# Neighbour sums of a graph layer in two levels: 32-column one-hots in four column strips, then units added per tile

## The chip, the cores and the metric

The kernel runs on one core of one Trainium2 chip. The metric is the device time of one execution in microseconds (us), as a median over runs. A core has a matrix engine (TensorE, rows marked PE; its weight loads are marked PEld), a vector engine (VectorE, DVE), a scalar engine (ScalarE, ACT), GpSimd (POOL), which also issues the indirect DMAs, and a sync engine (SP) that issues plain DMAs. The engines run their own streams in order and meet at semaphores.

## The reference, cut to what matters

There are N = 6250 nodes with D = 512 features, and E = 100000 edges whose `dst` is sorted. With `xn` the layer norm of `x`:

```
deg = max(segment_sum(1, dst), 1)
agg = segment_sum(xn[src], dst)                  # the part that changes
gnn = xn @ W1.T + b1 + (agg / deg) @ W2.T + b2
mix = linear attention over all nodes (16 heads): relu(q), relu(k), v, then a projection
x   = x + gnn + mix
x   = x + ffn(layernorm(x))                      # 2 of 8 experts, chosen once for all nodes
```

## The kernel before

Nodes are worked in T = 49 tiles of 128 rows. Numbers are carried as pairs of fp16 (a high part and a low part), so a product of two pairs is three fp16 matmuls for each 128 of the contraction (`three`: the high weights times high and low of the other side, lines L549 and L550, then the low weights times high, L554). A matmul here has 128 x 128 stationary values and 512 moving columns unless told otherwise.

**The first stage** (loop `for i in range(-1, T + 2)`, called the K stage below) normalizes the tiles, stores each one's fp16 pair as 128 rows of 2 KB to a table in HBM, and computes the attention's keys and a 512 x 512 sum: 12 + 12 matmuls a tile (`three` for the key, L708 to L710 for the sum). Preparation work of the weights and the edge lists is put between its iterations by `STEPS`. One of these steps, `below`, counts for every tile which block of 128 edges is its first one.

**A short middle** builds the attention's matrix from that sum (L759 to L772).

**The layer stage** runs `layer(i)` for i = 1 to 51. Iteration i holds the query of tile i (L742, L743, L747), for tile i-1 the transposes (L793 and L800), `three` with `wg1`, `three` with `wg2` (these take the tile's aggregate) and `three` with `wm`, and for tile i-2 the transpose of the new normalized row (L838). That makes 48 matmuls of 512 columns and 12 transposes a tile. It also holds the aggregation of a tile `ahead = i + skew`; skew is 3 at first and falls to 0 (`LAYERS`), as iterations without an aggregation are put in. Tiles 0 to 2 are aggregated in the K stage (`EARLY`: i = 39, 42, 45) and tile 3 in the middle.

**The expert stage** follows and is not touched.

**The aggregation.** GpSimd gathers the edges' source rows from the table: one indirect DMA for each block of 128 edges (`fetch`, L522), 784 of them, into a ring of R = 16 slots of 128 x 1024 fp16. SP waits for the slots' DMAs and passes each four on as `arrived`. VectorE makes one-hots of 128 edges x 128 nodes, four blocks at a time (`one_hot`, L1238: is the edge's `dst` the node's number?). TensorE multiplies: `add` is two matmuls for each block, one-hot times high half (L622) and low half (L623), into `ps_agg` (bank 6), all blocks of a tile into the same 128 x 512 sums. A block with edges of two tiles is multiplied in both. A `group` of four blocks ends with a matmul of one column (`nothing`, L610) that carries a semaphore; when it is done, GpSimd may fill the four slots again (`released`). The sum's last column is the degree (each table row ends in a constant): VectorE takes its reciprocal (`degrees`, L1268 and L1271), and ScalarE copies the scaled sum to SBUF (`keep_ah`, L961).

The gathers begin when the last table row is stored. The ring is the only thing that lets GpSimd run ahead of TensorE.

Of the kernel before, what the change touches and what calls it, by code (L numbers as in the profile page):

```python
# [16 lines left out]
ALU = mybir.AluOpType  # L17
# [14 lines left out]
U = 4  # L32
NULL = U // 2
COLS = (NULL + BLOCKS + (E % P == 0) + R - 1) // R * R
ROUNDS = COLS // R
RG = R // U
OG = 6
GROUPS = COLS // U
CH = (BLOCKS + P - 1) // P
FULL = BLOCKS // P  # L40
XI = 6
NS = 4
# [30 lines left out]
def after(eng, sem, count):  # L73

    if not isinstance(count, int) or count > 0:
# [8 lines left out]
EARLY = {39: 0, 42: 1, 45: 2}  # L84
LAYERS = ((1, 4, 3), (4, 12, 3), (12, 13, None), (13, 24, 2), (24, 25, None), (25, 36, 1), (36, 37, None), (37, T, 0),
          (T, T + 3, None))

# [7 lines left out]
STEPS.update({15: [("dst", 0), ("dst", 1)], 16: [("src", 0), ("src", 1)], 17: [("below", 0)]})  # L95
# [12 lines left out]
def raw_read(t):  # L108

    s = t + OFF  # L110
    if t >= T - NS:
        return 0
    for k, first in enumerate(RAW):
        if k and first <= s < first + C:
            return ORDER.index((k, C - 1)) + 1
    return ORDER.index(("below", 0)) + 1 if EDGES <= s < RAW[G2] else 0


def layers(eng, body):

    for lo, hi, skew in LAYERS:
        a, b = -(-lo // SLOTS), hi // SLOTS
        if lo < 4 or b <= a:
            a = b = hi // SLOTS + 1
        for i in range(lo, min(a * SLOTS, hi)):
            body(i, skew, i % SLOTS)
        if b > a:
            with eng.Fori(a, b) as g:
                for k in range(SLOTS):
                    body(g * SLOTS + k, skew, k)  # L130
            for i in range(b * SLOTS, hi):
                body(i, skew, i % SLOTS)


def program(nc, x, src, dst, gw1, gb1, gw2, gb2, qkv_w, proj_w, proj_b, attn_w, attn_b, gate_w, gate_b,
            w1, b1, w2, b2, out):
    ctx = ExitStack()
    with ctx:
# [3 lines left out]
        table = nc.dram_tensor("table", (N, 2 * D), F16, kind="Internal").ap()  # L142
        x2_dram = nc.dram_tensor("x2_rows", (ROWS, D), F32, kind="Internal").ap()
# [15 lines left out]
        below = edges[:, 4 * CH * P:].bitcast(F16)[:, 0:CH * (T + 1)].rearrange("p (a f) -> p a f", a=CH)  # L159
# [18 lines left out]
        firsts, uns = ring32[:, 15, 0:T + 1], ring32[:, 15, T + 1:2 * (T + 1)]  # L178
        before = ring32[:, 15, 2 * (T + 1):2 * (T + 1) + CH].bitcast(I32)
# [3 lines left out]

        onehot = sb("onehot", [P, OG * U, P], F16)
        oh32 = onehot[:, :, :].rearrange("p a f -> p (a f)").bitcast(F32)
        plb = oh32[:, 0:C * P].rearrange("p (a f) -> p a f", a=C)
# [1481 lines left out]
```

## Time and profile before

| | |
|---|---|
| median of 3 runs | 1579.8 us (1578.48 to 1582.28) |
| the profiled execution's span | 1578.3 us |
| TensorE busy | 1519.8 us (96%) |
| GpSimd busy | 799.0 us (51%), 753.5 us of it gathers |
| VectorE, ScalarE busy | 1003.1 us (64%), 604.5 us (38%) |
| mean DMA rate | 196 GB/s |

The profile gives no separate time of its own for the profiled execution beside its span. The span lies 1.5 us under the median, and I treat that as what lies around it. "Busy" of an engine is the time covered by its instructions. A matmul is shown with its full length from first column in to last column out (about 0.38 us), while the next one starts about 0.2155 us after it, so a busy TensorE need not be a full one: distances between starts tell more.

### The profile page before, as it was taken

The numbers are of one execution on the slowest core, as the hardware profiler recorded it, in microseconds if no ns is written. First come the engines' busy times: TensorE is split into PE (matmuls) and PEld (weight loads), VectorE is DVE, ScalarE is ACT, GpSimd is POOL, SyncE is SP. The second block draws the span as 40 slices with busy tenths as digits, with TensorE's granted clock in tenths as the row PEclk, the third lists the DMA queues.
The fourth block names the chain that finished last, engine by engine and source line by source line (L and its number), as shares of the span: only waits on it lengthen the run. The fifth ranks groups of instructions, "written<-read, shape, count | busy, mean of one in ns | idle before, by whom it ended". The sixth has DMA issues, their size and how long they took to land.

```text
span 1578.3 us, 29172 instructions
## 1 busy us (share of the span) xinstructions
PE 1519.8 (96%) x7597; PEld 733.7 (46%) x7598; DVE 1003.1 (64%) x2154; ACT 604.5 (38%) x997; POOL 799.0 (51%) x847
## 2 busy tenths in 40 slices
PE   5999999989999999999999999999999989999997
PEld 2444444444544444444444444444544444444443
DVE  7576522246666667666677666666666666666777
ACT  5777721111333333332333333333333335555554
POOL 4122143646777767777767777767777710000000
PEclk8999999999999999999999999999999989999998
DMA  9977776957777767777767777767777723322323
GB/s 237 262 170 190 189 179 132 217 151 208 234 235 234 234 209 231 234 234 237 233 206 239 239 240 233 234 209 236 236 233 233 233 80 120 107 90 96 106 87 112
DMA packets 166610, 308.64 MB, mean 196 GB/s; under 512 B 71986, under 2 KB 74572, under 8 KB 166260
## 3 DMA queue, kind: packets, MB, share of 16 engines
q0 software_dynamic: 62720, 205.57, 44.3%
q1 hardware_dynamic: 36112, 58.90, 11.7%
q10 hardware_dynamic: 67684, 42.96, 10.7%
q8 instruction: 53, 0.87, 0.2%
q14 instruction: 41, 0.34, 0.1%
HBM read 255.02 MB, written 39.49 MB: 187 GB/s over the span
## 4 chain that ended last, share of the span: by engine, by line
PE 70%; POOL 14%; issue 6%; DVE 3%; DMA 1%; ACT 0%; DVEq 0%; SPq 0%; ACTq 0%
POOL ring L522 14%; PE bank L549 13%; PE bank L554 13%; PE bank L550 12%; PE bank L622 8%; PE bank L623 8%; PE bank L708 2%; PE bank L709 2%; PE bank L710 2%; PE bank L742 2%; PE bank L747 2%; PE bank L743 2%; PE bank L793 1%; PE bank L838 1%; PE bank L800 1%
## 5 line engine op out<-in xcount | busy, mean ns | idle before, releaser
L522 POOL DMA_INDIRECT ring<-table,src_col x784 | 753.5, 961 | 328.9 <-issue 254.5
L622 PE MATMUL bank<-ring,onehot 128*128 x830 | 316.1, 381 | 14.8 <-issue 6.2
L623 PE MATMUL bank<-ring,onehot 128*128 x830 | 315.5, 380 | 0.0
L1238 DVE TENSOR_TENSOR onehot<-bank,dst_col 128x512 f32 x244 | 168.8, 692 | 96.5 <-issue 61.1
L961 ACT ACTIVATE work<-bank,rd 128x512 f32<-128x512 f32 x49 | 33.7, 687 | 336.4 <-DVE rd L1271 336.3
L549 PE MATMUL bank<-wts,xT 128*128 128x512 f16 x392 | 149.1, 380 | 4.1 <-DVE wts L1313 4.1
L550 PE MATMUL bank<-wts,xT 128*128 128x512 f16 x392 | 149.0, 380 | 0.0
L549 PE MATMUL bank<-wts,work 128*128 128x512 f16 x392 | 148.2, 378 | 0.2 <-DVE work L1441 0.2
L550 PE MATMUL bank<-wts,work 128*128 128x512 f16 x392 | 148.3, 378 | 0.0
L622 PEld LDWEIGHTS bank<-ring,onehot 128*128 x830 | 80.9, 97 | 126.5 <-issue 45.6
L623 PEld LDWEIGHTS bank<-ring,onehot 128*128 x830 | 81.1, 98 | 84.8 <-issue 0.9
L554 PE MATMUL bank<-wts,xT 128*128 128x512 f16 x392 | 101.5, 382 | 0.0
L554 PE MATMUL bank<-wts,work 128*128 128x512 f16 x392 | 100.6, 379 | 0.0
L1052 ACT ACTIVATE std<-mv,epsc 128x1 f32<-128x1 f32 x49 | 14.4, 295 | 222.6 <-DVE mv L1437 222.6
L1268 DVE TENSOR_SCALAR dg<-bank 128x1 f32<-128x1 f32 x49 | 7.7, 158 | 137.2 <-PE bank L610 137.2
L1118 ACT ACTIVATE work<-work 128x512 f32<-128x512 f32 x98 | 61.8, 630 | 79.9 <-DVE work L1622 78.8
L509 POOL TENSOR_TENSOR work<-work 128x512 f16<-128x512 f32 x27 | 31.7, 1176 | 119.8 <-ACT work L1015 119.8
L1013 ACT ACTIVATE work<-bank 128x512 f32<-128x512 f32 x49 | 29.2, 596 | 136.0 <-PE bank L554 131.6
L1622 DVE SCALAR_TENSOR_TENSOR work<-bank,mix,work 128x512 f32<-128x512 f32 x98 | 69.9, 747 | 15.1 <-PE bank L554 9.8
L1612 DVE SCALAR_TENSOR_TENSOR ring<-work,gexp,ring 128x512 f32 (+1 forms) x98 | 73.3, 748 | 8.9 <-DVE ring L1612 3.8
L549 PE MATMUL bank<-xT,wts 128*128 (+2 forms) x208 | 75.0, 367 | 3.1 <-ACT wts L1096 3.1
L708 PE MATMUL bank<-work,xT 128*128 128x512 f16 x180 | 69.6, 386 | 6.0 <-POOL work L509 6.0
(284 smaller groups left out, 2732.5 us busy)
## 6 DMA issues: line engine op xcount, KB each, us to landing
ring<-table,src_col POOLq DMA_INDIRECT x784, 3.7
x_rows<-work ACTq DMA_DIRECT2D x49, 256.0 KB, 3.7
work<-in_x ACTq DMA_DIRECT2D x48, 256.0 KB, 4.3
ring<-x_rows SPq DMA_DIRECT2D x12, 1024.0 KB, 5.3
out_x<-ring SPq DMA_DIRECT2D x12, 1024.0 KB
table<-xT SPq DMA_DIRECT2D x45, 256.0 KB, 3.5
ring<-in_x SPq DMA_DIRECT2D x42, 256.0 KB, 3.7
xT<-in_L_mix_qkv_weight SPq DMA_DIRECT2D x2, 1024.0 KB, 10.1
```

Source lines behind the costliest of these rows:

```text
L522: pool.indirect_dma_start(ring[:, n, :], None, table[:, :], bass.IndirectOffsetOnAxis(ap=ap, axis=0)).then_inc(slot_loaded[n], 16)
L549: mm(out_, wh(c), mh(c), start=first and c == 0, stop=False)
L550: mm(out_, wh(c), ml(c), start=False, stop=False)
L554: r = mm(out_, wl(c), mh(c), start=False, stop=last and c == n - 1)
L622: mm(ps_agg[:, :], w[:, k, :], rows[:, k, 0:D], start=start, stop=False, skip_group_check=True)
L623: r = mm(ps_agg[:, :], w[:, k, :], rows[:, k, D:2 * D], start=False, stop=stop, skip_group_check=True)
L708: mm(bank[c][:, :], xs[:, c * P:(c + 1) * P], kh, start=(t == 0), stop=False)
L961: F(ah[:, k % SLOTS, :], ps_agg[:, :], ACT.Copy, scale=rd[:]).then_inc(s["ah_made"], 1)
L1118: F(act2[:, j % 2, e], pre[:, j % 2, e], ACT.Gelu).then_inc(s["act_made"], 1)
L1238: V.tensor_tensor(onehot[:, bass.ds((q + t) % OG * U, U), :], ps_iota[:, None, :].to_broadcast([P, U, P]), dst_col[:, bass.ds(q % GROUPS * ...
L1612: r = V.scalar_tensor_tensor(out=y, in0=act2[:, j % 2, e], scalar=gexp[:, e:e + 1], in1=y, op0=ALU.mult, op1=ALU.add)
L1622: V.scalar_tensor_tensor(out=pre[:, j % 2, e], in0=bank[4 + 2 * (j % 2) + e][:, :], scalar=mix[:, 4:5], in1=b2b[:, e], op0=ALU.mult, op1=A ...
```

## The change

The blocks' sums are made in two levels. Blocks are taken three at a time as a *window* (384 edges; about 24 nodes by the mean degree of 16). `base[w]` is the first node of window w, and a one-hot is 128 edges x 32 nodes, relative to that base. Four windows (12 blocks) make a *unit*; there are 66 units. Window j of a unit uses column strip j of TensorE's array: its one-hot is 32 stationary columns at column 32 j, and its sums go to partitions 32 j to 32 j + 31 of `ps_unit` (bank 7). A *step* is one block of each of the four windows: two passes (high, low) of four matmuls, 197 steps in all (195 of four blocks, 2 of one). Three steps fill a unit. ScalarE then copies it to SBUF as the high fp16 half, VectorE makes the low half, into one of 6 unit slots. A tile's sum is then made from the 2 to 4 units that can hold its nodes (16 tiles have 4, 32 have 3, one has 2; 162 in all), with 128 x 128 one-hots (`keys`) that match node numbers: two matmuls for each unit, into the same `ps_agg` as before.

What else it does: the lists of first blocks and the loops with bounds read at run time go, `layer` is unrolled, and SP no longer relays arrivals (TensorE waits on one of four semaphores per step). The steps begin in the K stage at i = 33, one in each iteration (18 of them), 6 are put into the middle, and 173 into the layers by a plan (`PLAN`) at five places of each. Tiles 0 to 2 are summed at i = 40, 46 and 48 of the K stage. Skew falls to 0 at layer 23 instead of 37. The gathers of step n wait for step n-4. 782 blocks are gathered, not 784. The preparation step `below` gives way to three steps `first`, with a list built by VectorE (`make_lists`). If the lists are unsorted or spread too far (a window over more than 32 nodes, or a first node over 48 from its even place), the kernel takes a slower way first (`slow_tiles`). The descriptor memory of GpSimd's DMAs is set to 4096 bytes in place of its default of 16384.

What that test reads in the inputs: `dst` is sorted, the widest gap between first nodes of windows is 28, and the largest distance from the even place is 18. So the slower way is not taken.

```diff
-U = 4
+LANES, DEEP, WIDE = 4, 3, 32
+RG = R // LANES
+UB = LANES * DEEP
+UNITS = (BLOCKS + UB - 1) // UB
+STEP = P * DEEP * N // E // 8 * 8
+SPREAD = LANES * STEP
+DRIFT = 48
+HOLD = 6
-EARLY = {39: 0, 42: 1, 45: 2}
-LAYERS = ((1, 4, 3), (4, 12, 3), (12, 13, None), (13, 24, 2), (24, 25, None), (25, 36, 1), (36, 37, None), (37, T, 0),
+FIRST = 33
+TILES_K = {40: 0, 46: 1, 48: 2}
+LAYERS = ((1, 12, 3), (12, 13, None), (13, 17, 2), (17, 18, None), (18, 22, 1), (22, 23, None), (23, T, 0),
           (T, T + 3, None))
+def units_of(t):
+    lo = max(0, -(-(P * t - DRIFT - SPREAD) // SPREAD))
+    return range(lo, min(UNITS - 1, (P * t + P - 1 + DRIFT) // SPREAD) + 1)
 # in step_plan, the count of steps at place p (0 to 4) of layer i; n steps are out already
+            if t is not None and p < 3:
+                count = -(-(need - n) // (3 - p))
+            else:
+                count = 1 if n < more else 0
 # GpSimd
-            for b in range(COLS):
-                if b % U == 0:
-                    pool.wait_ge(s["released"], b // U + 1)
-                fetch(b % R, src_col[:, b:b + 1])
+            for n in range(STEPS_SUM):
+                u, k = divmod(n, DEEP)
+                after(pool, s["step_done"], n - RG + 1)
+                for j in lanes_of(n):
+                    b = UB * u + DEEP * j + k
+                    fetch(slot(n, j), src_col[:, b:b + 1], step_loaded[n % RG])
 # TensorE
-            def group(q, t, part=None, f=None):
...
+            def add_step(n):
+                u, k = divmod(n, DEEP)
+                last = n + 1 == steps_to(u)
+                pe.wait_ge(step_loaded[n % RG], 16 * sum(len(lanes_of(m)) for m in range(n % RG, n + 1, RG)))
+                if k == 0:
+                    pe.wait_ge(s["hot_made"], u + 1)
+                    after(pe, s["unit_lo"], u)
+                for h in range(2):
+                    for j in lanes_of(n):
+                        a = j * WIDE
+                        r = mm(ps_unit[a:a + WIDE, :], hot[:, u % 2, DEEP * j + k, :], ring[:, slot(n, j), h * D:(h + 1) * D],
+                               start=(k == 0 and h == 0), stop=(h == 1 and k == DEEP - 1 or last), skip_group_check=True,
+                               tile_position=(0, a))
+                r.then_inc(s["step_done"], 1)
+            def add_units(t):
+                us = units_of(t)
+                after(pe, s["ah_made"], t)
+                after(pe, s["dg_made"], t)
+                pe.wait_ge(s["keys_made"], t + 1)
+                pe.wait_ge(s["unit_lo"], us[-1] + 1)
+                for j, u in enumerate(us):
+                    mm(ps_agg[:, :], keys[:, t % 2, j, :], units[:, u % HOLD, 0:D], start=(j == 0), stop=False)
+                    r = mm(ps_agg[:, :], keys[:, t % 2, j, :], units[:, u % HOLD, D:2 * D], start=False, stop=(u == us[-1]))
+                r.then_inc(s["agg_made"], 1)
 # ScalarE
+            def unit_high(u):
+                act.wait_ge(s["step_done"], steps_to(u))
...
+                F(units[:, u % HOLD, 0:D], ps_unit[:, :], ACT.Copy, scale=SU).then_inc(s["unit_hi"], 1)
 # VectorE
-                V.tensor_tensor(onehot[:, bass.ds((q + t) % OG * U, U), :],
-                                ps_iota[:, None, :].to_broadcast([P, U, P]),
-                                dst_col[:, bass.ds(q % GROUPS * U, U), None].to_broadcast([P, U, P]),
-                                ALU.is_equal).then_inc(s["oh_made"], 1)
+            def make_hot(u):
...
+                V.tensor_tensor(hot[:, u % 2, 0:w, :], iota16[:, None, 0:WIDE].to_broadcast([P, w, WIDE]),
+                                rel_col[:, b:b + w, None].to_broadcast([P, w, WIDE]), ALU.is_equal
+                                ).then_inc(s["hot_made"], 1)
+            def make_keys(t):
+                after(dve, s["agg_made"], t - 1)
+                for j, u in enumerate(units_of(t)):
+                    r = V.tensor_scalar(keys[:, t % 2, j, :], iota16[:], tile_base[:, t:t + 1], node[:, u:u + 1],
+                                        ALU.add, ALU.is_equal)
+                r.then_inc(s["keys_made"], 1)
+            def unit_low(u):
+                dve.wait_ge(s["unit_hi"], u + 1)
+                V.scalar_tensor_tensor(out=units[:, u % HOLD, D:2 * D], in0=ps_unit[:, :], scalar=SU,
+                                       in1=units[:, u % HOLD, 0:D], op0=ALU.mult, op1=ALU.subtract).then_inc(s["unit_lo"], 1)
+                if u + 2 < UNITS:
+                    make_hot(u + 2)
```

## Rows read from the trace of the kernel before

**Rows 1.** The page's costliest groups: the gathers and one of the aggregation's two matmul lines.

```profile
L522 POOL DMA_INDIRECT ring<-table,src_col x784 | 753.5, 961 | 328.9 <-issue 254.5
...
L623 PE MATMUL bank<-ring,onehot 128*128 x830 | 315.5, 380 | 0.0
```

**Rows 2.** Line L522's summary: durations in ns and starts in us; then its idle.

```profile
L522 POOL DMA_INDIRECT ring<-table,src_col x784: 940/946/1447, 209.1 to 1268.5; - x196
...
  issue: 254.5, 764
  PE bank L610: 72.5, 14
  PE bank L623: 1.8, 6
...
DMA to landing us min/median/max: 3.3/3.7/8.6
```

**Rows 3.** GpSimd's instructions in order of time, K stage: start, duration, idle before.

```profile
209.14 1.12 POOL L522 DMA_INDIRECT ring<-table,src_col  x1 [22.09 <-issue]
...
253.12 0.94 POOL L522 DMA_INDIRECT ring<-table,src_col  x1 [23.06 <-PE bank L610]
254.36 0.94 POOL L522 DMA_INDIRECT ring<-table,src_col  x1 [0.30 <-issue]
```

**Rows 4.** TensorE in order of time, one layer of the steady stage.

```profile
706.75 0.19 PE L610 MATMUL bank<-ones,zero 128*128 128x1 f16 x2
706.80 0.63 PE L793 MATMUL bank<-ident,work 128*128 128x128 f32 x4
707.27 0.60 PE L800 MATMUL bank<-ident,work 128*128 128x128 f32 x4
707.73 0.39 PE L622 MATMUL bank<-ring,onehot 128*128 x1
...
711.22 1.03 PE L554 MATMUL bank<-wts,xT 128*128 128x512 f16 x4
712.08 0.38 PE L622 MATMUL bank<-ring,onehot 128*128 x1
```

**Rows 5.** Summary of line L1379, once for each tile.

```profile
L1379 DVE SCALAR_TENSOR_TENSOR work<-bank,ksb x49: 681/691/692, 349.8 to 1270.8; 128x512 f32<-128x512 f32 x49
```

**Rows 6.** Busy time by stretch: engines, granted clock, DMA share, GB/s.

```profile
core 0: us, PE busy (x) PEld busy (x) DVE busy (x) ACT busy (x) POOL busy (x), PEclk, DMA share, GB/s
...
340.00:358.00 18.00, 11.81 (x49) 5.20 (x47) 9.85 (x27) 3.11 (x5) 13.74 (x15) 1.00 0.72 207
...
520.00:1160.00 640.00, 634.95 (x3289) 311.82 (x3288) 435.43 (x958) 201.91 (x303) 472.33 (x494) 1.00 0.76 231
```

**Rows 7.** TensorE in order of time at the start of layer 1.

```profile
358.74 0.63 PE L623 MATMUL bank<-ring,onehot 128*128 x1
359.17 0.63 PE L622 MATMUL bank<-ring,onehot 128*128 x1
```

**Rows 8.** ScalarE in order of time: the key's copy, iterations 33 and 34 of the K stage.

```profile
220.93 0.60 ACT L1013 ACTIVATE work<-bank 128x512 f32<-128x512 f32 x1 [4.09 <-PE bank L554]
226.11 0.60 ACT L1013 ACTIVATE work<-bank 128x512 f32<-128x512 f32 x1 [4.09 <-PE bank L554]
```

**Rows 9.** Groups by line and shape, 520 to 1160 us: busy, mean ns, idle before.

```profile
L1238 DVE TENSOR_TENSOR onehot<-bank,dst_col 128x512 f32 x152 | 105.2, 692 | 59.1 <-issue 37.5 <-DVE bank L1246 12.8 <-PE bank L610 5.6
...
L1444 DVE SCALAR_TENSOR_TENSOR work<-bank,work 128x512 f16<-128x512 f32 x34 | 23.1, 681 | 0.0
...
L961 ACT ACTIVATE work<-bank,rd 128x512 f32<-128x512 f32 x31 | 21.3, 687 | 223.5 <-DVE rd L1271 223.5
```

**Rows 10.** Summary of line L1268, which ends each tile's aggregation.

```profile
L1268 DVE TENSOR_SCALAR dg<-bank x49: 147/159/160, 271.3 to 1277.6; 128x1 f32<-128x1 f32 x49
```

**Rows 11.** VectorE and GpSimd in order of time, steady stage.

```profile
677.89 0.74 DVE L1486 SCALAR_TENSOR_TENSOR work<-work,e 128x512 f32<-128x512 f32 x1
678.30 1.15 POOL L522 DMA_INDIRECT ring<-table,src_col  x1 [0.30 <-issue]
```

More of the change, by code:

```diff
@@ L41 @@
 XI = 6
+HOLD = 6
+SU = 2.0 ** -8
 NS = 4
@@ L115, in raw_read @@
             return ORDER.index((k, C - 1)) + 1
[L116 to L132, printed above, removed]
+    return ORDER.index(("first", 2)) + 1 if EDGES <= s < RAW[G2] else 0
 def program(nc, x, src, dst, gw1, gb1, gw2, gb2, qkv_w, proj_w, proj_b, attn_w, attn_b, gate_w, gate_b,
@@ L529, in _, with fetch @@
[L529 to L530 removed]
+            many = slow_tiles(pool)
+            def fetch(k, ap, sem):
+                pool.indirect_dma_start(ring[:, k, :], None, table[:, :],
+                                        bass.IndirectOffsetOnAxis(ap=ap, axis=0)).then_inc(sem, 16)
+            with pool.If(many > 0):
+                with pool.Fori(0, many) as t:
                     with pool.Fori(0, ROUNDS) as g:
[L532 to L533 removed]
+                        it = t * ROUNDS + g
+                        pool.wait_ge(s["slow_half"], it * 2 + 1)
@@ L801, in layer @@
                     r.then_inc(s["turned_p"], 1)
-                if ahead is not None:
-                    with pe.If(a + 1 < b):
-                        group(a + 1, ahead)
-                t = i - 1
+                steps_at(1)
                 if real(t):
                     after(pe, s["x2_made"], t)
-                    if isinstance(t, int) and t == 0:
+                    if t == 0:
                         pe.wait_ge(s["matrix_split"], 2)
@@ L839, in layer @@
                     r.then_inc(s["turned_x2"], 1)
-            layers(pe, layer)
+            for i in range(1, END):
+                layer(i)
             warm(3)
@@ L932, in prepare @@
             def prepare(n, kind, c):
-                if kind in ("scale", "below"):
+                if kind in ("scale", "first"):
                     act.wait_ge(s["steps_act"], n)
@@ L1437, in layer @@
                     V.bn_aggr(mv, st6[:]).then_inc(s["mv2_made"], 1)
+                for u in ends(i, 0):
+                    unit_low(u)
                 t = i - 1
@@ L1477, in layer @@
                     weigh(t)
+                for u in ends(i, 1, 2):
+                    unit_low(u)
                 t = i - 2
```

640 lines of the change are left out of this document (359 added, 281 removed).

## The prediction

> **What bounds the kernel now.** I read the page first: its share of busy time says TensorE (96%), with 1660 matmuls of the aggregation (two lines of 830) as the largest term [rows 1]. Then I looked at how GpSimd issues its gathers, since they feed these matmuls. A gather is shown with 0.946 us and is followed by 0.30 us of "issue", so they come every 1.25 us even when nothing holds them [rows 3]. Over all, (753.5 + 254.5 - 22.1) / 784 = 1.2575 us each [rows 1, 2]; the 22.1 us is the idle time ahead of the first one [rows 3]. The waits on TensorE (lines L610 and L623) are only 72.5 + 1.8 = 74.3 us in total [rows 2]. Check: 209.1 + 784 x 1.2575 + 74.3 = 1269.3, and the last gather starts at 1268.5 and takes 0.95 [rows 2].
>
> So there are two bounds, one just behind the other. TensorE needs 19.19 us a tile ((1270.8 - 349.8) / 48, rows 5 being one event for each tile: [rows 5]). GpSimd needs 782 / 49 = 15.96 blocks x 1.2575 = 20.07 us a tile. GpSimd is the slower one in the steady stage, where it is never held, and lives on the lead it has from the K stage. The lead is small because of the ring: 16 gathers from 209.1, then 23 us of waiting for tile 0's aggregation [rows 3], and so on three times more.
>
> What is to be seen: taking matmuls from TensorE is worth, in this kernel, at most the 74 us in which GpSimd waited, and not the time of the matmuls.
>
> **The change: TensorE's work.** Matmuls of 512 columns start 0.2155 us apart: four of L554 take from 711.22 to 712.08 [rows 4]. A tile has 48 of them, 10.34 us, and 12 transposes: L793's four and L800's take 0.47 and 0.46 us to the next start [rows 4], with L838's as many, 1.4 us. The aggregation is 830 / 49 x 2 = 33.9 matmuls [rows 1], 7.3 us. Sum 19.1 against the 19.19 measured.
>
> Removed: 1660 x 0.2155 = 358 us, and the one-column matmuls. Added for the units: 162 x 2 x 0.2155 = 70 us, 1.5 us a tile with the wait. Added for the steps: 197 times s, the time of one step. No row shows four matmuls in column strips, so I bound it. Below: the four of a pass run together, 2 x 0.2155 = 0.43 us. Above: they run one after the other, 8 x 0.2155 = 1.72 us. I take **s = 0.8**: two passes, and 0.17 us of refill on either side for the change of shape, by the difference between a matmul's length (0.38) and its pitch (0.2155) [rows 1, 4]. A tile then costs TensorE 10.34 + 1.4 + 1.5 + 4.02 x 0.8 = 16.5 us, which is less than GpSimd's 20.07; 197 x 0.8 + 70 = 228 us replace 358.
>
> The Trainium skill, "TensorEngine Tiling (Array Packing)", Key Properties, says that a change of tiling mode drains TensorE, which speaks against two changes for each step of eight short matmuls; no row here shows one. By "TensorE: Matmul & The Clock Gate", Part 3, three column tiles gave 2.38x; carried to four (an estimate from that page, 3.2x) a pass would take 0.27 us and a step 0.54, and the sum below would be some 9 us lower. The same part says that weight loads overlap matmuls in flight only where their row groups differ; here all four strips use all rows, which would make the strips run in turn (the second rival).
>
> **The change: the other engines.** VectorE loses 152 / 640 x 19.19 = 4.6 one-hots of 0.69 us a tile [rows 9], 3.2 us. It gains 1.33 units x (0.68 for the low half, as L1444, and 0.6 for 12 x 32 one-hots, 384 of L1238's 512 elements) and 3.3 keys, each at most half a one-hot of L1238, 0.34: 2.8 us. It was busy 435.4 of 640 us [rows 6] and stays below. ScalarE gains 1.33 x 0.69 us (as L961, rows 9: [rows 9]) where it was busy 202 of 640 us. Both are hidden by GpSimd's pace. Their place matters: one bank holds the unit in the making, so a unit's first step waits for both copies of the one before, 0.69 + 0.68 and some 0.4 between engines, 1.8 us; but steps lie 5.03 us (four gathers) apart where gathers bound, and that covers it. If TensorE were the bound, 65 x 1.8 us would partly show. The lists cost VectorE some 5 us more at i = 12 to 17, where normalization runs many tiles ahead, so 0. Seven fp32 products of 128 columns on TensorE there cost at most 1.3 us (0.12 to 0.2 each), all ahead of the gathers: **+1.3**. SP's relay goes, worth at most 0.3 us a step where TensorE waits for a gather: inside the landing time below. The smaller descriptor memory changes nothing unless it holds fewer than the four or so gathers in flight (landing 3.7 us over a pitch of 1.25, [rows 2]); then the gathers' pitch would grow, which is part of the third rival.
>
> **The change: when gathers may start.** The first gather moves to 209.1 + 1.3 = 210.4. The K stage's iteration lasts 5.18 us (226.11 - 220.93) [rows 8]. Step 0 comes after the key of tile 33, at 222.2, and later iterations last 5.18 + 0.8 = 5.98 us. Four gathers last 5.03 us, and those of step n wait for step n-4, so the ring's lead of four steps is eaten up at about n = 13. The middle holds six steps in about as much time as it had with tile 3's blocks, and layer 1 starts near 354 (before, matmuls of layer 1 are under way at 358.7, [rows 7]). Step 24 stands late in layer 1: 354 + 3 x 2.6 + 1 + 0.8 = 363.7. Step 28's gathers can't start before it; unheld they would start at 210.4 + 28 x 5.03 = 351.2. **12.5 us** are lost by then, in place of nearly all the 74. After layers 12 and 22, which sum no tile, TensorE has some 18 us of other work between two steps, with a ring of 20 us less 3.7 of landing: 4.0 + 3.5 us lost, and 1.4 in small ones. In sum 21.4. Elsewhere TensorE is the faster (16.5 against 20.07), so it takes each step as it lands.
>
> The last gather ends at 210.4 + 782 x 1.2575 + 21.4 = **1215.1**, against 1269.5 before: 54.4 us earlier.
>
> **The change: behind the last gather.** Before, the last aggregation ended at 1277.6 [rows 10], 8.1 us behind the last gather. Now the plan gives layers 3, 3 and 6 steps in turn, and 6 to layer 46, 3 to layer 47, 0 to layer 48. Layer 46's last step lands 7.5 us before the end of the last gather, plus 3.7: 1211.3. Then step, units and transposes 3.1, layer 47 at TensorE's pace (10.34 + 1.45 + 2.4 + 1.4 = 15.6), and layer 48 up to its units (10.34 + 0.95 + 1.4 = 12.7): 1242.7. That is 27.5 us behind the last gather, so **19 us are given back**. What follows (layers 49 to 51, experts: 1578.3 - 1277.6 = 300.7 us) is the same work in the same order. Span: 1242.7 + 300.7 = 1543.4; with the 1.5 us to the median, **1545 us**, 35 under the 1580 shown.
>
> **The likeliest one's own range.** s = 0.45 takes off 12 us (gather stalls 10 in place of 21, less in the last layers); s = 1.2 adds 20. A gather pitch of 1.2475 (0.946 + 0.30, no contention) takes off 8. So 1526 to 1565.
>
> **Rivals.**
> 1. *The strips are nearly free and gathers smooth*: s near 0.45 and the low pitch, 1526 to 1532. Within the likeliest.
> 2. *The strips run in turn* (the other side). s = 1.72: TensorE then needs 13.3 + 6.9 = 20.2 us a tile, plus the copies' 1.8 us wherever two steps meet across a unit. By the same sum the stalls are 98 us and the end is 1628. This mechanism decides from s = 1.4 on, where it comes to 1578. For it: nothing in the trace shows strips side by side. Against it: TensorE works through the small shapes it has at less than its pitch for 512 columns (one-column matmuls of L610 in pairs within 0.05 us, [rows 4]), so small pieces don't each cost a full slot. Neither settles s. (The rule on weight loads from Part 3 of the TensorE page of the Trainium skill, named above, would bring this about; no row here shows it.) 12 in 100.
> 3. *Gathers grow slower.* A gather is 15 ns over its shortest in the mean, 12 us in all, and a long one (1.15 us) falls beside VectorE's L1486, which reads two SBUF operands [rows 11], as others do. The new one-hots read two SBUF operands; the old ones read PSUM and one. If the excess doubles, +12: 1557; were each new one-hot to hold a gather by its own 0.6 us, 66 x 0.6 = 40 us: 1585. 10 in 100, 1557 to 1585.
> 4. *TensorE's clock falls in the starved layers.* Every third layer has six steps and lasts 29 us with some 18 us of work, idle 3 to 4 us at a time. In 340 to 358 TensorE was busy 11.8 of 18 us, and from 358.4 to 361.7 matmuls started 0.43 us apart, the lower of its two levels (1.2 GHz in place of 2.4) [rows 6, 7]. While it waits for gathers this costs nothing; what reaches into the next two layers, at 15.6 us against 15.1 us of gathers, costs half of such a stretch, 1.7 us, up to 13 times: +22, 1567. 10 in 100.
> 5. *No change*: TensorE's waits (a unit's copies behind long queues on VectorE and ScalarE, 1.5 to 3 us a layer) bring it to 19.2 us a tile again: 1575 to 1583. 6 in 100.
> That the change doesn't run as written (its slower way) is excluded by the inputs.
>
> **Chances.** Likeliest 58 (with rival 1), rival 2 12, rival 3 10, rival 4 10, rival 5 6, and 4 for something slower unnamed. Taking 0.2% (3 us, about what this kernel's runs can tell): faster 58 + 10 + 10 + 2, less 1 for rival 3's upper end, 79; the same 5; slower 16. The range 1522 to 1585 leaves out rival 2 and some 6 more.
>
> **What the new profile should show.** A gather pitch of 1.25 to 1.26 us from 210 on with under 30 us of waits on TensorE in total, most of them before 370; last gather at 1205 to 1225; strips of a pass starting a few ns apart and a step of 0.5 to 1.2 us; TensorE waiting on gathers in every third layer; last `dg` at 1230 to 1255, then 300.7 us. Wrong it would be by a step of over 1.4 us, a pitch over 1.27, or a tail after the last `dg` that isn't 300 us.

## The result and the profile after

The changed kernel takes 1563.95 us (median of 4 runs, 1555.31 to 1565.38), against 1580.96 us for the kernel before, measured beside it: ratio 0.9882, 95% interval 0.9856 to 0.9909. So it is 1.2% faster, where 2.2% was predicted. The profiled execution has a span of 1561.7 us (predicted 1543.4) and took 1563.55.

The page of the changed kernel, its busy shares, its shares of the chain that ended last, the gathers' group that answers to [rows 1], and the group of the steps' matmuls. Columns as there.

```profile
PE 1388.8 (89%) x7490; PEld 619.8 (40%) x7490; DVE 933.8 (60%) x2172; ACT 640.9 (41%) x1063; POOL 799.5 (51%) x849
...
POOL 39%; PE 30%; issue 13%; DVE 3%; DMA 3%; ACT 1%; SPq 0%; DVEq 0%; ACTq 0%; POOLq 0%
...
L609 POOL DMA_INDIRECT ring<-table,src_col x782 | 753.5, 963 | 282.0 <-issue 255.3
...
L724 PE MATMUL bank<-ring,hot 128*32 128x512 f16 x1564 | 127.4, 403 | 123.2 <-DMA ring<-table,src_col 101.3
```

The same chain of the kernel before:

```profile
PE 70%; POOL 14%; issue 6%; DVE 3%; DMA 1%; ACT 0%; DVEq 0%; SPq 0%; ACTq 0%
```

TensorE's busy share fell from 96% to 89%, and the chain that ended last now runs over GpSimd's gathers (39%, 14% before) more than over TensorE (30%, 70% before). TensorE waits 101.3 us for gathered rows, where it waited 2.3 us for SP's word of them before: the bound has passed from one engine to the other.

The summary of the gathers' line of the changed kernel, answering to [rows 2].

```profile
L609 POOL DMA_INDIRECT ring<-table,src_col x782: 940/946/1438, 220.1 to 1232.4; - x196
its engine sat idle before it (us, times) until:
  issue: 255.3, 766
  PE bank L724: 26.7, 16
...
DMA to landing us min/median/max: 3.4/3.8/15.2
```

The waits on TensorE are 26.7 us (74.3 before, 21.4 predicted). Ahead of the first gather lie 22.24 us of idle, so a gather takes (753.5 + 255.3 - 22.2) / 782 = 1.2616 us (1.2575 predicted). The first one starts at 220.1 and not at 210.4.

The summary of the line that ends each tile's aggregation, for the changed kernel, answering to [rows 10].

```profile
L1405 DVE TENSOR_SCALAR dg<-bank x49: 146/158/159, 279.3 to 1261.3; 128x1 f32<-128x1 f32 x49
```

The last gather ends at 1232.4 + 0.95 = 1233.3. The last aggregation comes 28.0 us behind it (27.5 predicted), and 1561.7 - 1261.3 = 300.4 us follow (300.7 predicted).

Busy time in the stretch of [rows 6], changed kernel.

```profile
520.00:1160.00 640.00, 552.40 (x3249) 240.67 (x3242) 392.38 (x967) 225.68 (x344) 481.99 (x501) 0.95 0.78 234
```

TensorE is busy 552 of 640 us (635 before). GpSimd issues 501 gathers in place of 494, 1.4% more: this small number is the whole steady gain. In this stretch the gathers waited 20.5 us on TensorE before (19.3 on L610, 1.2 on L623) and wait 7.2 now; those 13 us are more than the 9 us that seven gathers take. The granted clock is 0.95 in place of 1.00.

TensorE in order of time in one layer, changed kernel, answering to [rows 4].

```profile
453.39 1.03 PE L658 MATMUL bank<-wts,xT 128*128 128x512 f16 x4
454.35 0.61 PE L724 MATMUL bank<-ring,hot 128*32 128x512 f16 x8
454.90 0.66 PE L852 MATMUL bank<-ident,work 128*128 128x128 f32 x4
```

A whole step, eight matmuls of 512 columns in four strips, takes 454.90 - 454.35 = 0.55 us. The estimate worked out from the Trainium skill, "TensorE: Matmul & The Clock Gate", Part 3, by carrying its factor for three column tiles to four, was 0.54, and the trace agrees. Two passes that each take the pitch of one matmul are 2 x 0.2155 = 0.43, so both changes of shape together cost some 0.12 us.

### Where the missing 18 us are

The span is 18.3 us over the predicted one. Term by term, from the rows above: gathers' start +9.7 (220.1 for 210.4), pitch +3.2 (782 x 0.0041), waits on TensorE +5.3, tail +0.5, rest -0.3. Sum 18.4. The largest is the start, which I had put at +1.3 us and which came to +11.0.

ScalarE in order of time, K stage of the changed kernel: L1082 is the key's copy that was L1013. The first five lines are iterations 14 to 18; the last one is iteration 33.

```profile
120.86 0.60 ACT L1082 ACTIVATE work<-bank 128x512 f32<-128x512 f32 x1
129.32 0.60 ACT L1082 ACTIVATE work<-bank 128x512 f32<-128x512 f32 x1 [2.25 <-PE bank L658]
135.26 0.60 ACT L1082 ACTIVATE work<-bank 128x512 f32<-128x512 f32 x1 [2.41 <-PE bank L658]
147.11 0.60 ACT L1082 ACTIVATE work<-bank 128x512 f32<-128x512 f32 x1 [7.23 <-PE bank L658]
152.73 0.60 ACT L1082 ACTIVATE work<-bank 128x512 f32<-128x512 f32 x1 [2.28 <-PE bank L658]
...
231.74 0.60 ACT L1082 ACTIVATE work<-bank 128x512 f32<-128x512 f32 x1 [4.09 <-PE bank L658]
```

The same copies of the kernel before:

```profile
118.59 0.60 ACT L1013 ACTIVATE work<-bank 128x512 f32<-128x512 f32 x1 [0.30 <-PE bank L554]
124.97 0.60 ACT L1013 ACTIVATE work<-bank 128x512 f32<-128x512 f32 x1 [0.17 <-PE bank L554]
130.92 0.60 ACT L1013 ACTIVATE work<-bank 128x512 f32<-128x512 f32 x1 [2.42 <-PE bank L554]
136.30 0.60 ACT L1013 ACTIVATE work<-bank 128x512 f32<-128x512 f32 x1 [0.77 <-PE bank L554]
141.92 0.60 ACT L1013 ACTIVATE work<-bank 128x512 f32<-128x512 f32 x1 [1.73 <-PE bank L554]
```

The lag behind the kernel before is 2.3 us at the first line, 4.3 at the second and third, and then 10.8 at the fourth, where it stays up to iteration 33 (231.74 against 220.93, [rows 8]). Two pieces of work stand at these places. The first is on VectorE:

```profile
113.72 3.17 DVE L1313 TENSOR_SCALAR xT<-ident,xT 128x128 f32<-128x128 f32 x7
117.11 0.75 DVE L1300 SCALAR_TENSOR_TENSOR wts<-bank,scale,wts 128x512 f16<-128x512 f32 x1 [0.21 <-DVE xT L1313]
```

The seven products are 3.17 us long, and the split of the weights stands behind them in VectorE's queue (at 117.11; 114.45 in the kernel before). The second is on TensorE, where the three `first` steps come in one iteration. In order of time, TensorE's wait behind the first piece, and its wait at the second:

```profile
121.90 0.52 PE L698 MATMUL bank<-ident,xT 128*128 128x128 f32 x3 [3.03 <-ACT wts L1003]
...
139.72 0.46 PE L670 MATMUL bank<-xT,ones 128*128 128x128 f32 x2 [3.16 <-ACTq L987]
```

The three matmuls of L698 in the first line start at 119.24 in the kernel before, after 0.25 us of idle. The profile names ScalarE's queue, which acknowledges each such step (L987), as what ended the second wait.

Behind both waits matmuls start 0.43 us apart, the lower of the two clock levels: from 123.1 to 126.5 and from 140.3 to 143.7. In the kernel before they start 0.2155 us apart at these places. Eight such distances cost 1.7 us more than at the higher level. So the lag of 10.8 us is 2.7 us at the first piece and 1.7 us of lower clock behind it, then 4.8 us at the second (the longer products, and the wait) and 1.7 us of lower clock again. This account is read from the start times.

### The profile page after: what moved, and what is told of

The parts are those of the page before. It is cut to its first block, busy times and chain, and to the rows that moved or that the text cites. A ratio compares the mean times of both kernels' runs of the same rounds, so it can differ in the third digit from the quotient of the medians.

```text
span 1561.7 us, 22443 instructions
## 1 busy us (share of the span) xinstructions
PE 1388.8 (89%) x7490; PEld 619.8 (40%) x7490; DVE 933.8 (60%) x2172; ACT 640.9 (41%) x1063; POOL 799.5 (51%) x849
## 3 DMA queue, kind: packets, MB, share of 16 engines
q10 hardware_dynamic: 67684, 42.96, 10.8%
## 4 chain that ended last, share of the span: by engine, by line
POOL 39%; PE 30%; issue 13%; DVE 3%; DMA 3%; ACT 1%; SPq 0%; DVEq 0%; ACTq 0%; POOLq 0%
POOL ring L609 39%; PE bank L653 8%; PE bank L658 8%; PE bank L654 8%; PE bank L776 2%; PE bank L778 2%; PE bank L777 2%; DMA ring<-table,src_col 1%; DMA xT<-awb 1%; PE bank L724 1%; DMA work<-in_x 1%; DVE ring L1754 1%; DVE work L1764 0%; PE bank L737 0%; PE bank L738 0%
## 5 line engine op out<-in xcount | busy, mean ns | idle before, releaser
L609 POOL DMA_INDIRECT ring<-table,src_col x782 | 753.5, 963 | 282.0 <-issue 255.3
L653 PE MATMUL bank<-wts,xT 128*128 128x512 f16 x588 | 234.3, 398 | 6.4 <-DVE wts L1452 3.3
L724 PE MATMUL bank<-ring,hot 128*32 128x512 f16 x1564 | 127.4, 403 | 123.2 <-DMA ring<-table,src_col 101.3
L654 PE MATMUL bank<-wts,xT 128*128 128x512 f16 x588 | 233.8, 398 | 0.0
L658 PE MATMUL bank<-wts,xT 128*128 128x512 f16 x588 | 156.4, 390 | 0.0
L724 PEld LDWEIGHTS bank<-ring,hot 128*32 128x32 f16 x1564 | 24.5, 95 | 209.3 <-DMA ring<-table,src_col 144.0
L658 PE MATMUL bank<-wts,work 128*128 128x512 f16 x392 | 101.3, 381 | 0.0
L1361 DVE SCALAR_TENSOR_TENSOR units<-bank,units 128x512 f16<-128x512 f32 x66 | 45.6, 691 | 78.6 <-ACT units L1013 78.5
L653 PEld LDWEIGHTS bank<-wts,xT 128*128 128x128 f16 x588 | 59.6, 101 | 80.9 <-issue 24.0
L658 PEld LDWEIGHTS bank<-wts,xT 128*128 128x128 f16 x588 | 59.3, 101 | 75.3 <-issue 10.4
L1082 ACT ACTIVATE work<-bank 128x512 f32<-128x512 f32 x49 | 29.2, 596 | 143.0 <-PE bank L658 132.3
L654 PEld LDWEIGHTS bank<-wts,xT 128*128 128x128 f16 x588 | 59.8, 102 | 64.2 <-issue 9.9
L1013 ACT ACTIVATE units<-bank 128x512 f16<-128x512 f32 x66 | 38.7, 586 | 112.9 <-PE bank L724 104.0
```

Source lines behind the costliest of these rows:

```text
L609: pool.indirect_dma_start(ring[:, k, :], None, table[:, :], bass.IndirectOffsetOnAxis(ap=ap, axis=0)).then_inc(sem, 16)
L653: mm(out_, wh(c), mh(c), start=first and c == 0, stop=False)
L654: mm(out_, wh(c), ml(c), start=False, stop=False)
L658: r = mm(out_, wl(c), mh(c), start=False, stop=last and c == n - 1)
L724: r = mm(ps_unit[a:a + WIDE, :], hot[:, u % 2, DEEP * j + k, :], ring[:, slot(n, j), h * D:(h + 1) * D], start=(k == 0 and h == 0), stop=( ...
L1013: F(units[:, u % HOLD, 0:D], ps_unit[:, :], ACT.Copy, scale=SU).then_inc(s["unit_hi"], 1)
```

## The experiments

Theory A, as the expectations call it: the strips run side by side, GpSimd's gathers are the bound of the layers, and the end is start of the gathers + 782 pitches + their waits + tail + 300 us.

### 1. Is it the strips, and is it the gathers?

Each kernel of this part ran once, with one run of the kernel before beside it (1577.22 us).

**All four windows on strip 0.** The sums of the four windows then fall on the same 32 partitions; the count and shape of the matmuls stay.

```diff
-                        a = j * WIDE
+                        a = 0
```

> All four windows of a step use column strip 0 and its 32 partitions instead of a strip each (the sums are then not the reference's); all else as in the changed kernel. Theory A, that strips run side by side and that this is what frees TensorE: matmuls in one strip start 0.2155 us apart, a step takes 1.7 us instead of 0.54, TensorE needs some 20.2 us a tile and becomes the bound; 1625 to 1650 us. Rival, that the gathers set the time whatever a step costs: within 10 us of the changed kernel's 1564.

1661.11 us. TensorE in order of time, this kernel:

```profile
601.88 1.90 PE L724 MATMUL bank<-ring,hot 128*32 128x512 f16 x8
603.71 0.39 PE L653 MATMUL bank<-wts,work 128*128 128x512 f16 x1
```

The step takes 603.71 - 601.88 = 1.83 us in place of 0.55, 3.3 times as long. So four strips do run side by side, and this kernel is what rival 2 described: the gathers now wait 132.1 us on TensorE. The time is 33 us above the 1628 worked out for s = 1.72, and 11 above the 1625 to 1650 expected here; the longer step (1.83) explains a part of it, the rest was not traced.

**Half of the gathers.** Only two of the four lanes of a step are fetched; the other two multiply the same rows again, so TensorE's work is whole, while lanes 2 and 3 are summed from the rows of lanes 0 and 1. (TensorE's wait for a step then counts two lanes; that line is left out below.)

```diff
-                for j in lanes_of(n):
+                for j in lanes_of(n)[0:2]:
...
-ring[:, slot(n, j), h * D:(h + 1) * D],
+ring[:, slot(n, j % 2), h * D:(h + 1) * D],
```

> The changed kernel with only the gathers of lanes 0 and 1 of each step; lanes 2 and 3 multiply the rows of 0 and 1 again, so TensorE's work is the same and the sums are not the reference's. Theory A, that GpSimd's issue of gathers is the bound: 15.5 us a tile are left for TensorE, last aggregation some 200 us earlier or less by the K stage's share, total 1390 to 1440 us. Rival, that TensorE's waits for VectorE and ScalarE (a unit's two copies, queues of the layer) keep the layers near 19 us: 1520 to 1560 us.

1441.83 us, 122 less and 2 above the range expected. TensorE now is the bound: the gathers wait 436.8 us for it. Its aggregations number 23 from 757.0 to 1126.0, so 22 distances of 16.8 us a tile, where I had worked out 16.5 (with the measured step in that sum 15.5, so its other terms were 1.3 us short).

**Half of the gathers in the kernel before**: odd blocks are summed from the rows of the even ones. (The edits to `add` and to SP's waits that belong to this are left out below.)

```diff
-                fetch(b % R, src_col[:, b:b + 1])
+                if b % 2 == 0:
+                    fetch(b % R, src_col[:, b:b + 1])
```

> The kernel before with only every second block gathered; TensorE multiplies the rows of the even slots twice, so its work is the same and the sums are not the reference's. Theory A, two bounds close together: TensorE alone keeps 19.1 us a tile, so 1565 to 1580 us, 0 to 15 under the kernel before. Rival, that GpSimd was the sole bound before: under 1540 us.

1560.54 us against 1577.22 beside it: 4 under the range that two close bounds were given, and far from the rival's 1540. Halving the gathers was worth 17 us before the change and 122 after it: TensorE bound the kernel before, with GpSimd close behind it, and now GpSimd comes first.

**The small descriptor memory in the kernel before.**

```diff
-    nc = _bacc.Bacc("TRN2", target_bir_lowering=False, num_devices=1)
+    nc = _bacc.Bacc("TRN2", target_bir_lowering=False, num_devices=1, dynamic_dma_scratch_size=4096)
```

> The kernel before with the descriptor memory of GpSimd's DMAs at 4096 bytes as in the changed kernel. Theory A, that it holds more than the gathers in flight: gathers keep (busy + issue) / 784 = 1.2575 us, 1577 to 1583 us. Rival, that it is what took the pitch to 1.2616 in the changed kernel: 1.261 or more and 3 us longer waits of TensorE.

1581.21 us; the gather's pitch is (749.3 + 254.7 - 22) / 784 = 1.253 us. So the small memory is not what made 1.2575 into 1.2616.

### 2. The gathers' start and the tail

**Cheap lists**: one product in place of seven, and the third `first` step an iteration later.

```diff
-STEPS.update({15: [("dst", 0), ("dst", 1)], 16: [("src", 0), ("src", 1)], 17: [("first", 0), ("first", 1), ("first", 2)]})
+STEPS.update({15: [("dst", 0), ("dst", 1)], 16: [("src", 0), ("src", 1)], 17: [("first", 0), ("first", 1)], 18: [("first", 2)]})
...
-                for k in range(CH):
-                    link(V.tensor_scalar(steps[:, k, :], ident[:], f_dst[:, k, 0:1], None, ALU.mult))
+                link(V.tensor_tensor(steps, ident[:, None, :].to_broadcast([P, CH, P]),
+                                     f_dst[:, :, 0:1].to_broadcast([P, CH, P]), ALU.mult))
```

> The changed kernel, with the seven products for the step matrices made in one wider product on VectorE, and the third list step of the first group moved one iteration later. Theory A (the gathers set the end, so their late start is paid in full): the first gather goes from 220.1 back to about 210 to 212, the last one ends about 8 to 10 us earlier (1233.3 becomes 1223 to 1225), the time is 1553 to 1556. Rival B (the start is hidden, the tiles' matmuls or the transposes of the first stage set the end): first gather earlier, but the waits of the gathers on TensorE and on the tile inputs grow by the same 8 to 10 us, the time stays at 1561 to 1564. Rival C (the start is not late because of these two edits): the first gather stays at 218 to 220, no change.

1553.43 us, ratio to before 0.9819 (0.9784 to 0.9854). The same places in its trace, VectorE's product, ScalarE's copy of iteration 17, the gathers (a fence for each view):

```profile
113.80 1.09 DVE L1313 TENSOR_TENSOR xT<-ident,xT 128x896 f32<-128x896 f32 x1
```

```profile
138.09 0.60 ACT L1083 ACTIVATE work<-bank 128x512 f32<-128x512 f32 x1 [1.90 <-PE bank L659]
```

```profile
L610 POOL DMA_INDIRECT ring<-table,src_col x782: 943/949/1461, 211.3 to 1220.8; - x196
its engine sat idle before it (us, times) until:
  issue: 254.5, 763
  PE bank L725: 23.2, 19
```

The copy is at 138.09, 9.0 us earlier; the first gather at 211.3, 8.8 earlier. TensorE's first wait is 0.95 us in place of 3.03, the second is gone, and no matmul here starts at the lower clock's distance. What was won at the start came through whole: the last gather is 11.5 us earlier, which is the 8.8 and 3.5 us less of waits on TensorE, less 0.8 us of longer pitch. The time is 10.5 less. By the ratios, 0.9819 against 0.9882, it is 10 us, with intervals that just don't touch; rivals B and C are out by the first gather and the waits, not by the time alone.

**DRIFT 24** in place of 48, so that a tile takes fewer units (130 pairs of key matmuls in place of 162), and layer 46 has three steps, layer 47 six.

```diff
-DRIFT = 48
+DRIFT = 24
...
-                count = -(-(need - n) // (3 - p))
+                count = max(0, -(-(need - n) // (3 - p)))
```

> The changed kernel, with 24 blocks in place of 48 between a tile and the units that it may use, so that the units' plan runs less far ahead: 130 additions of a unit to a tile's sum in place of 162, and the last layer has less to do behind the last gather. Theory A (the end is last gather plus what the last tiles need): gathers start and end as before, the last aggregation is 22 to 25 us behind the last gather in place of 28, the time is 1558 to 1561. Rival B (the plan's shift only moves the waits of the gathers on TensorE, the tail is set by the last layers' own chain): 1562 to 1565. Rival D (fewer steps in late layers lets the gathers' waits on TensorE, 26.7, fall too): 1553 to 1558.

1552.41 us, 0.9812 (0.9795 to 0.9828): 11.5 us less, more than any theory had. In its trace the last gather ends at 1232.4 and the last aggregation is at 1254.3, 21.9 us behind: the tail gives 6.1 (theory A's mechanism), the waits are 27.9 and did not fall (so not theory D's), the span (1553.6) is 8.1 lower, and the rest of the 11.5 is within the spread of the runs: the profiled execution, 1555.38, was the slowest of its four.

**Both.**

> Both edits (cheap lists and 24 blocks of drift). Theory A says that they add, since one moves the gathers' start and the other what follows their end: 1548 to 1552. If one of them is covered by the other's wait (rival B), it is no better than the better one alone, 1553 or more.

1544.44 us, 0.9756 (0.9736 to 0.9776). Better than either theory's time. They add, nearly: -19.5, singly -10.5 and -11.5. In the trace the start is 8.6 us earlier (8.8 alone) and the tail 5.1 shorter (6.1 alone).

**Both, and gathers three iterations earlier**, the rows' norms made at two tiles an iteration from i = 18 so that they are there in time.

```diff
-FIRST = 33
+FIRST = 30
...
-        more = steps_to(units_of(nxt)[-1])
+        more = steps_to(units_of(min(nxt + 1, T - 1))[-1])
```

> Both edits, and the gathers begin after tile 30 of the first stage in place of tile 33, with the rows' sums made at two tiles per iteration so that the lists are there; the plan of the steps looks one tile further. Three iterations of 5.2 us earlier: first gather at 195 to 200. Theory A (the gathers at 1.26 us each, one behind the other, set the end): all of it comes through less what the longer overlap with the first stage costs, 1530 to 1540. Rival B (in the first stage the gathers wait for the tiles' transposes and TensorE, so what starts earlier only waits longer there): the waits within the first stage grow by 10 us or more, and the time is that of the kernel with both edits or above, 1545 to 1555.

1530.16 us, 0.9675 (0.9658 to 0.9691), the fastest. Its gathers and its last aggregation:

```profile
L612 POOL DMA_INDIRECT ring<-table,src_col x782: 940/946/1407, 200.0 to 1203.1; - x196
its engine sat idle before it (us, times) until:
  issue: 239.3, 757
  PE bank L727: 20.8, 25
```

```profile
L1408 DVE TENSOR_SCALAR dg<-bank x49: 150/158/160, 272.6 to 1226.8; 128x1 f32<-128x1 f32 x49
```

The first gather is 11.5 us earlier than with both edits alone (211.5), not the 15.6 of three iterations, and the time 14.3 us less: within theory A's range. The gathers' waits fell from 25.6 to 20.8 us, where rival B had them grow by 10.

### 3. The waits that are left: dealing the steps evenly

The plan gives 3, 3 and 6 steps in turn. A three-step layer frees 12 slots, 15.1 us of gathers, and by my sum takes TensorE slightly longer. So four in each layer might end the waits.

**Even, and ahead of need**: at most 1, 2, 2, 3, 4 steps are out at the five places of a layer, whether needed or not.

```diff
...
-                count = 1 if n < more else 0
+            if not count and n < min(max(more, 4 * (i + 1) + LEVEL), base + (1, 2, 2, 3, 4)[p], STEPS_SUM):
```

> The changed kernel with its steps dealt out evenly: four per layer in place of three, three and six in turn. Theory E (the gathers' 26.7 us of waits on TensorE come from the three-step layers, which free only 12 blocks of the ring in the 16.5 us or more that TensorE needs for a layer, 15.1 us of gathers): these waits fall to 10 to 15 us, what is left being the first stage's, the last gather ends 10 to 15 us earlier, time 1549 to 1555; TensorE's clock in the late layers is no lower than 0.91 since no layer is left waiting for two layers' worth of rows. Rival F (the waits come from the first stage and from the layers without a tile, not from the dealing): waits stay at 22 to 28 us and the time at 1560 to 1565. Rival G (a layer now waits for its fourth step's rows where it waited for three, so the last aggregation comes later than 28 us behind the last gather): above 1565.

1567.83 us, 0.9911 (0.9894 to 0.9927): slower than the changed kernel, though its gathers end sooner.

```profile
L610 POOL DMA_INDIRECT ring<-table,src_col x782: 941/946/1472, 219.0 to 1223.3; - x196
its engine sat idle before it (us, times) until:
  issue: 254.0, 762
  PE bank L725: 18.4, 20
```

```profile
L1406 DVE TENSOR_SCALAR dg<-bank x49: 145/158/159, 278.2 to 1264.6; 128x1 f32<-128x1 f32 x49
```

The last gather ends at 1224.2, 9.1 us earlier, and the last aggregation comes 40.4 us behind it in place of 28.0. So the waits did fall, by 8.3 us (to 18.4, where theory E had 10 to 15), and rival G, which put the loss behind the last gather, was right on the time. The granted clock in stretches of 80 us from 760 to 1240 was 0.91 at the lowest, as theory E had it (0.87 in the changed kernel). The reason for the tail is in the plan: the last steps stand in layer 46 and not in 47, so one more layer is left when the rows run out. The kernel with steps dealt late, below, tests this.

> The kernel with both edits and the earlier gathers (1530.2), with four steps per layer. Theory E: its 20.8 us of gathers' waits on TensorE fall to about 10, time 1518 to 1524. Rival F: 1528 to 1532.

The same dealing in the fastest kernel: 1542.37 us, 0.9753 (0.9730 to 0.9776), where both E and F had said 1532 or less. Waits 12.3 us (20.8), last gather 1198.2 (1204.1), tail 42.3 (22.7).

**Even, but late**: a step is taken when the even line needs it, so that the last four stand in layer 47.

```diff
...
-                count = -(-(need - n) // (3 - p))
+                count = max(0, -(-(min(max(need, 4 * t + EVEN), STEPS_SUM) - n) // (3 - p)))
...
```

> The changed kernel with about four steps per layer, but no step taken earlier than the sums need it (the last four steps in layer 47, where the changed kernel has its last three, and not in layers 45 and 46 as in the first even dealing, which gave 1567.8). Theory H (what the even dealing won at the gathers, 9 us, it paid behind them, because steps taken ahead of need leave one layer more of work behind the last gather): gathers wait 16 to 20 us on TensorE, last gather ends at 1222 to 1226, the last aggregation follows 26 to 30 us later, time 1552 to 1557. Rival I (evenness itself makes the layers wait for their rows, so the tail stays near 40 us): 1563 to 1568.

1552.72 us, 0.9808 (0.9791 to 0.9824), 15 less than the other even dealing. Last gather 1225.2, tail 25.1: theory H holds here. Its waits are 23.0, a little more than expected.

> The kernel with both edits and the earlier gathers (1530.2, and 1542.4 with steps run ahead), now dealt evenly and late. Theory H: waits about 12 to 15 us, last gather ends near 1198 to 1200, last aggregation 22 to 25 us later, time 1522 to 1527. Rival I: 1538 to 1543.

1538.94 us, 0.9733 (0.9686 to 0.9780). Here H missed by 12 us: the tail is right (24.3), but the waits are 27.9 in place of 12 to 15. The waits of this kernel in 520 to 760 us, and below them those of the fastest kernel in the same stretch:

```profile
  PE bank L727: 12.1, 4
```

```profile
  PE bank L727: 0.6, 2
```

In this stretch lie the layers without a tile and those after them, which this dealing gave two steps each, and the ring filled. The fastest kernel gives layers 17 and 22 five steps. That these layers are the cause is read from the plan and the stretch; it was not tried by itself.

## Why the prediction was right, and twice as large as the gain

All kernels with the strips side by side and all rows fetched, from their traces (us; last gather is its end, tail the way from there to the last aggregation, rest the way from there to the end of the span). The time alone is the median of the runs, and need not be that of the execution in the trace:

| kernel | first gather | waits on TensorE | last gather | tail | rest | time |
|---|---|---|---|---|---|---|
| changed | 220.1 | 26.7 | 1233.3 | 28.0 | 300.4 | 1563.95 |
| cheap lists | 211.3 | 23.2 | 1221.8 | 25.6 | 301.3 | 1553.43 |
| DRIFT 24 | 219.1 | 27.9 | 1232.4 | 21.9 | 299.3 | 1552.41 |
| both | 211.5 | 25.6 | 1221.3 | 22.9 | 300.7 | 1544.44 |
| both, early | 200.0 | 20.8 | 1204.1 | 22.7 | 300.5 | 1530.16 |
| even, ahead | 219.0 | 18.4 | 1224.2 | 40.4 | 301.1 | 1567.83 |
| even, ahead, early | 202.2 | 12.3 | 1198.2 | 42.3 | 299.7 | 1542.37 |
| even, late | 219.6 | 23.0 | 1225.2 | 25.1 | 300.6 | 1552.72 |
| even, late, early | 198.6 | 27.9 | 1211.2 | 24.3 | 304.1 | 1538.94 |

Last gather less first gather less waits, over 782, is 1.257 to 1.263 us in every row. The form of the prediction's sum (start + 782 pitches + waits + tail + rest) is thus the right one; its terms stand as follows.

- **What bounds.** Right for what the change would do: two bounds close together before, GpSimd well ahead as the bound after; halving the gathers was worth 17 and 122 us. One reading was wrong: that GpSimd was the slower one in the steady stage and never held there. It waited 20.5 us on TensorE in 520 to 1160 us. The 20.07 us a tile of the gathers were set against 19.19 us a tile of TensorE, but the second is a mean over 48 layers of which three sum no tile, so the two aren't like for like.
- **The step, s = 0.8.** 0.55 us measured, so it was taken too high by nearly half. In the kernel it mattered little: TensorE has slack in the layers, and the sum for a tile was too low elsewhere (16.8 us in the kernel with half the gathers). In the forecast it mattered more, and to its luck: by the prediction's own slope (12 us for 0.35 us of step) the right step would have given 1536, and the miss would have been 28 us and not 19. Also the upper edge of the likeliest range, 1565, was priced by a slower step (1.2 us); that 1563.95 lies under it has other causes, below.
- **The start of the gathers, +1.3 us: this is the step that failed.** I priced the seven products on TensorE and called the lists' 5 us on VectorE hidden, by the lead of the normalization. The price on TensorE was about right (in the kernel with cheap lists 12 of the 14 matmuls of these products take 1.33 us); the zero for what queues on VectorE and ScalarE was not. Measured +11.0: behind the 3.17 us of products on VectorE, and TensorE's wait of 3.03 us there, the key copies lag by 4.3 us, and behind the three `first` steps of one iteration, with a wait of 3.16 us, by 10.8. Some 3.4 us of this are the lower clock after the two waits. Undoing both pieces brought 8.8 us of the start and 10.5 us of time. The two were undone together: how the 11 us share between them, and with the clock, is read from start times and not tried one by one.
- **The pitch, 1.2575.** 1.2616, +3.2 us. Rival 3 made the new one-hots the cause; kernels with the same one-hots show 1.257 to 1.263, and the kernel before shows 1.2575 and, with the small descriptor memory, 1.253. The difference is as small as those between kernels with the same gathers, and nothing of it is shown to come from the change. Rival 3's price of 12 us or more is excluded.
- **The waits, 21.4.** 26.7, of which 19.2 in ten waits up to 333 us (12.5 predicted by layer 1) and 7.5 later (8.9 predicted). The right step would have made the forecast smaller here (10 us of waits at s = 0.45), so this term was worse than its 5 us of miss says. The K stage's iterations with a step last 5.83 us (5.98 predicted) against some 5.0 of four gathers; most waits there are 0.7 to 1.6 us, the usual 0.3 of issue in them. The last of the ten, 6.56 us, had a transposing DMA of tile 48 ahead of it, and is 1.56 us at this place in the trace of the first even dealing. So about 5 us of it may be of one execution.
- **The tail, 27.5, and the rest, 300.7.** 28.0 and 300.4. The 19 us given back were right, and they can be had back in part: 22.7 with a smaller DRIFT.
- **What the sum had covered.** A unit's first step waits for the copies of the unit before; I had this covered by the distance of the steps. It shows: TensorE waited ten times for VectorE's copy (L1361), 18.6 us in all. No run here tells what of it reaches the end.
- **Rival 4, the clock.** It fell in the layers, to 0.91 of full in 840 to 1000 us and 0.87 in 1080 to 1160, but the gathers' waits on TensorE are only 4.3 us in all of 760 to 1240, so at most that was lost to it there, against the 22 us of the rival. Rival 1 (1526 to 1532) was no bad picture of the strips, but its time needs what the fastest kernel has besides. Rival 2 is excluded by the step of 0.55 us, rival 5 by the change of bound.

## What to carry to other kernels

When an engine is relieved, ask which one is a few per cent behind it, and write the new end as that one's start + count x pitch + waits + what follows its last item; then every microsecond ahead of its first item costs a full one, also work that was free under the old bound. Preparation on another engine is hidden only if nothing of the stage is queued behind it: look for what is behind it in that queue, not at the engine's share. Work run ahead of need takes waits from the feeding engine but can leave one stage more behind its last item (a tail of 40.4 us in place of 28.0), so put consumption as late as the feed's buffer allows, at the end above all; too late elsewhere fills the buffer (27.9 us of waits in place of 20.8). And check a change on the terms of the sum, since errors of two terms can hide each other in the time.

## What the runs showed of the hardware

- Four matmuls of 32 columns in four column strips run side by side: a step of eight takes 0.55 us, and 1.83 us on one strip (8 x 0.229, against the 0.2155 of 128-column matmuls in [rows 4]). The Trainium skill, "TensorEngine Tiling (Array Packing)", Key Properties, has TensorE drained when the tiling mode changes; here two changes and eight matmuls together take 0.55 us, 0.12 above two bare passes. The Trainium skill, "TensorE: Matmul & The Clock Gate", Part 3, lets weight loads overlap matmuls in flight only where row groups differ; the trace doesn't agree for these strips, which share all rows: the eight loads of a step, 0.095 us each (0.76 in sum), are all shown within 0.12 us from 454.35, while the first matmuls run. The kernel before spoke against it too: in 520 to 1160 us weight loads cover 311.8 us beside matmuls that cover 635 of 640 [rows 6].
- An indirect gather of 128 rows costs GpSimd 0.944 to 0.949 us (median) and 0.30 us of issue in all of these kernels, 1.25 to 1.26 us each over 782 of them. With half of the gathers and a DMA share of 0.51 (757 to 1126 us) the median is 0.946 as well.
- A wait of 3 us on TensorE can cost more than itself: behind each of the two in the K stage eight matmuls started 0.43 us apart in place of 0.2155, 1.7 us more. Behind the wait of 0.95 us in the kernel with cheap lists they did not.
- With gathers running beside the K stage (DMA share 0.92 in 310 to 333 us), one DMA that transposes took 16.3 us to land, where the median of the others is 4.6:

```profile
310.81 16.30 DMA xT<-awb
```
